# Bias network in steps 1 to 11, masks by the group, 16 transposes of the identity ahead of x

## What is computed

```python
def rel_pos_bias(n, w0, b0, g0, w1, b1, g1, w2, b2, dtype):
    pos = jnp.arange(-n + 1, n, dtype=dtype)[:, None]
    h = jax.nn.silu(ln(pos @ w0 + b0, g0))
    h = jax.nn.silu(ln(h @ w1 + b1, g1))
    h = h @ w2 + b2
    ...
x = x + L0(x, bias=fside_16xSxS, mask=mask_bk0, null_kv=cond, ...)   # layernorm, q/k/v, softmax, Wo, layernorm
x = x + L1(x, bias=rel_pos_bias(...), mask=mask_bf1, ...)            # the same with l2norm of q and k
```

## Time and profile before

| | us |
|---|---|
| median of 3 runs | 1332.85 (1330.36 to 1334.3) |
| the profiled execution | 1334.16 |
| its span | 1332.4 |
| TensorE busy | 1284.4 (96%) |
| VectorE, ScalarE, GpSimd busy | 1101.6, 861.7, 797.3 |

### The profile page before, as it was taken

One profiled execution on the slowest core, in us unless ns is written; L12 is line 12 of the kernel. 1 busy time (PEld: TensorE's weight loads), 2 busy tenths in 40 slices (PEclk: granted clock), 3 DMA queues, 4 the chain that ended last, 5 costly groups with the idle time before them and its releaser, 6 DMA issues.

```text
span 1332.4 us, 28554 instructions
## 1 busy us (share of the span) xinstructions
PE 1284.4 (96%) x8152; PEld 1183.8 (89%) x8152; DVE 1101.6 (83%) x2948; ACT 861.7 (65%) x3246; POOL 797.3 (60%) x1382
## 2 busy tenths in 40 slices
PE   3798999999999999999999999999999999999997
PEld 2587999999999999999999999999999999999995
DVE  5676877877777887887799999899899999999986
ACT  3565667666667777776666766666666666666663
POOL 6443444444445666554567776776766766776673
PEclk8898999999999999999999999999999999999999
DMA  9101411111123212213454101101111110110101
GB/s 286 35 19 50 78 44 47 36 35 47 47 96 111 86 59 96 102 58 112 110 129 174 49 24 47 47 31 39 47 36 34 47 45 26 47 47 24 47 33 40
DMA packets 52195, 85.67 MB, mean 64 GB/s; under 512 B 7888, under 2 KB 22256, under 8 KB 51616
## 3 DMA queue, kind: packets, MB, share of 16 engines
q1 hardware_dynamic: 47168, 75.81, 18.2%
q0 software_dynamic: 4128, 9.03, 2.3%
q10 hardware_dynamic: 832, 0.04, 0.0%
HBM read 57.07 MB, written 27.79 MB: 64 GB/s over the span
## 4 chain that ended last, share of the span: by engine, by line
PE 92%; DVE 3%; issue 2%; ACT 1%; SPq 1%; POOL 1%; DMA 0%; POOLq 0%; DVEq 0%; ACTq 0%
PE bank_q L1270 30%; PE bank_y L1406 26%; PE bank_s L1270 12%; PE bank_o L1270 10%; PE bank_p L1371 6%; PE bank_t L1344 4%; PE bank_t L1310 3%; ACT p_raw L799 1%; PE bank_t L1349 1%; DVE wq_raw L969 1%; PE bank_y L1270 0%; POOL bias L569 0%; SPq L367 0%; DMA bias<-in_fside_16xSxS 0%; DVE pt_l L1152 0%
## 5 line engine op out<-in xcount | busy, mean ns | idle before, releaser
L799 ACT ACTIVATE p_raw<-s_sb,neg_m 128x130 f32<-128x130 f32 (+1 forms) x1024 | 372.0, 366 | 134.7 <-DVE neg_m L1142 133.0
L641 POOL TENSOR_TENSOR p_sb<-p_raw,rden 128x256 f32<-128x256 f32 x256 | 157.6, 615 | 308.3 <-DVE rden L1148 308.3
L1270 PE MATMUL bank_q<-wq_h,xt_h 128*128 128x384 f32 x768 | 268.2, 349 | 4.4 <-DVE xt_l L1040 4.3
L1270 PE MATMUL bank_q<-wq_h,xt_l 128*128 128x384 f32 x768 | 260.0, 339 | 0.0
L1270 PE MATMUL bank_q<-wq_l,xt_h 128*128 128x384 f32 x768 | 259.8, 338 | 0.0
L631 POOL TENSOR_TENSOR bias_g<-bias,mask_row 128x260 f32<-128x260 f32 x256 | 178.5, 697 | 120.7 <-DVE s_sb L1135 119.2
L1406 PE MATMUL bank_y<-wo_h,ot_h 128*128 128x512 f32 x512 | 218.0, 426 | 0.3 <-DVE ot_l L1158 0.3
L1406 PE MATMUL bank_y<-wo_h,ot_l 128*128 128x512 f32 x512 | 201.8, 394 | 0.0
L1406 PE MATMUL bank_y<-wo_l,ot_h 128*128 128x512 f32 x512 | 201.5, 394 | 0.0
L799 ACT ACTIVATION_READ_ACCUMULATOR p_raw<-s_sb,neg_m 128x1 f32 x1024 | 192.5, 188 | 0.0
L1152 DVE TENSOR_TENSOR pt_l<-bank_p,pt_h 128x384 fp32r<-128x384 f32 x256 | 140.6, 549 | 37.4 <-ACT pt_h L806 37.4
(11 more groups left out here) (136 smaller groups left out, 3155.3 us busy)
## 6 DMA issues: line engine op xcount, KB each, us to landing
x_in<-in_x SPq DMA_DIRECT2D x32, 256.0 KB, 3.1
x_res<-in_x SPq DMA_DIRECT2D x32, 256.0 KB, 2.7
x_mid<-y_out SPq DMA_DIRECT2D x32, 256.0 KB, 2.1
x_in<-x_mid SPq DMA_DIRECT2D x32, 256.0 KB, 2.8
x_res<-x_mid SPq DMA_DIRECT2D x32, 256.0 KB, 2.7
out_x<-y_out SPq DMA_DIRECT2D x32, 256.0 KB, 2.1
wq_raw<-in_L_cond_Wq SPq DMA_DIRECT2D x4, 768.0 KB, 6.4
wq_store<-w_sb SPq DMA_DIRECT2D x6, 384.0 KB, 3.9
```

The costliest lines, as they stand in the source:

```text
L641: e.tensor_tensor(to[:, 0:2 * P].rearrange("p (e j) -> p e j", e=2), low_blocks(of)[:, :, 2:LOW], r[:, 0:2, :].broadcast_to([P, 2, P]), AL ...
L799: last = e.activation(p_raw[:, g % 2, lo:hi], s_sb[:, g % 2, lo:hi], ACT.Exp, bias=neg_m[:, h:h + 1], accum_out=esum[:, h:h + 1])
L1270: last = e.matmul(out, a, b, start=(k == 0), stop=(k == len(passes) - 1))
```

## The change

- The bias network leaves the prologue and step 0. Its first layer runs in step 1, norm in 2, silu in 3 and 4 (exp in 3), transposes in 5, product (into `bank_t` now) in 6, second norm in 7, silu in 8 and 9, transposes in 10, table in 11, store in 12. w0, b0 and g0 lie in the upper columns of `wq_raw`, and are loaded once the weights are split. FIRST of layer 0 becomes 13, so that steps 0 to 12 are written out and the loop has steps 13 to 15.
- SP loads the mask ahead of bias0, no network rows ahead of the second x, and the third and fourth x in the prologue.
- GpSimd makes the second rstd ahead of never_seen and the null columns, masks bias0 a group at a time with masked_bias between, and makes the third rstd ahead of groups 2 and 3. Layer 1's null columns move to step 4.
- VectorE takes the second x's statistics and ln_apply around the third part of wq_l, writes the first null key before the splits, and takes the third x's statistics in step 0 (`third_x`).
- The first item's k is transposed into `bank_y` and its second q half into `bank_o`, k first.
- The first projections wait for each chunk of wq_l. wo_l chunks 0 to 3 are VectorE's in two pieces of step 0, chunks 4 to 7 GpSimd's in step 1.
- TensorE transposes the identity 16 times into a bank of scores before the first x.

```diff
-FIRST, LAST = 4, (15, B - 4)
+FIRST, LAST = (13, 4), (15, B - 4)
...
-        w0_b, b0_b, b1_b = row_of(p_raw), row_of(s_sb), wq_raw[:, 0, 0:D]
+        w0_b, b0_b, b1_b = wq_raw[:, 0, D:2 * D], wq_raw[:, 1, D:2 * D], wq_raw[:, 0, 0:D]
...
+        def bank_of_qt(m, half):
+            return bank_o if is_item(m, 0, 0) and half == 1 else bank_t
+        def bank_of_kt(m):
+            return bank_y if is_item(m, 0, 0) else bank_t
...
             load_x((0, 0))
             load_wq(0)
-            for dst, src in ((w0_b, w0[0]), (b0_b, b0), (g_b[0], g0)):
-                net_row(dst, src)
+            load_mask(0)
             load_bias0(0)
             wait(e, xn_ready, (0, 0))
             load_x((0, 1))
             load_bias0(1)
-            load_mask(0)
+            wait(e, xn_ready, (0, 1))
+            load_x((0, 2))
             load_wo(0)
+            net_load(w1_sb[:, :, :], w1.rearrange("(c p) n -> p c n", p=P))
...
+            wait(e, xn_ready, (0, 2))
+            load_x((0, 3))
             for p in range(3):
-                e.wait_ge(wq_ready[p], 1)
+                e.wait_ge(wq_ready[p], KC)
+            for dst, src in ((w0_b, w0[0]), (b0_b, b0), (g_b[0], g0)):
+                net_row(dst, src)
...
             load_small()
+            inverse_deviations(item_of(-2))
             never_seen()
             e.wait_ge(null_bias_loaded, 16 * LAYERS)
             place_nulls(0)
-            place_nulls(1)
-            mask_bias0()
-            inverse_deviations(item_of(-2))
+            mask_bias0(0)
+            masked_bias((0, 0), 0)
+            mask_bias0(1)
             masked_bias((0, 0), 1)
-            net_deviation(VE1)
-            masked_bias((0, 0), 0)
+            inverse_deviations(item_of(-1))
+            mask_bias0(2)
+            mask_bias0(3)
             masked_bias((0, 0), 2)
-            inverse_deviations(item_of(-1))
...
+            def third_x(m):
+                if is_item(m, 0, 0):
+                    x_stats((0, 2))
+                    means_variances(item_of(-1))
+            def net_part(m):
+                if is_item(m, 0, 1):
+                    net_first_layer()
+                if is_item(m, 0, 2):
+                    net_norm(RSTD1, CEN1, g_b[0])
+                if is_item(m, 0, 3):
+                    net_silu(EXP1, PLUS1, REC1, [0, 1])
+                if is_item(m, 0, 4):
+                    net_silu(EXP1, PLUS1, REC1, [2, 3])
+                if is_item(m, 0, 6):
+                    net_stats(PRE2, ST2, MV2)
...
                 on(0, maxima, 1)
+                on(0, third_x)
                 on(0, sums, 0)
...
                 on(1, split_qt, 0)
-                on(0, net_second_silu, [0, 1])
+                on(0, net_part)
                 on(0, split_pt, 1)
-                on(0, start_output)
                 on(3, x_stats)
                 on(0, sums, 3)
                 on(1, split_qt, 1)
                 on(0, split_pt, 2)
+                on(0, start_output, [0, 1])
...
             project_weights(0, 1)
-            project_weights(0, 2)
             x_stats(second)
             means_variances(item_of(-2))
+            project_weights(0, 2)
+            ln_apply(second)
+            first_null()
+            null_key(0)
             take_mask(first)
-            net_first_layer()
-            first_null()
             q_scale_out(first, 2)
-            ln_apply(second)
             split_qt(first, 0)
-            net_norm(RSTD1, CEN1, g_b[0])
+            split_kt(first)
             split_qt(first, 1)
-            net_silu(EXP1, PLUS1, REC1, [0])
-            split_kt(first)
-            x_stats(third)
-            means_variances(item_of(-1))
-            net_silu(EXP1, PLUS1, REC1, [1, 2, 3])
...
                 for c in range(KC):
-                    passes += [(xt_h[:, c, :], wq_h[:, c, lo:hi]), (xt_h[:, c, :], wq_l[:, c, lo:hi]),
+                    if is_item(m, 0, 0):
+                        e.wait_ge(wq_ready[p], c + 1)
...
+                    for b, done in ((6, TCOPY1), (7, PRE2), (11, TCOPY2), (12, TABLE)):
+                        if is_item(m, 0, b):
+                            e.wait_ge(net_step, done)
...
+            def idle_transposes(n):
+                for _ in range(n):
+                    e.transpose(bank_s[1][:, 0:P], ident[:, :], ident[:, :])
             first = (0, 0)
+            idle_transposes(16)
             transpose_x(first)
             for p in range(3):
                 project(first, p)
             transpose_q(first, 0)
+            transpose_k(first)
             transpose_q(first, 1)
-            transpose_k(first)
             stream(e, step)
```

More of the change, by code:

```diff
@@ L430, in bulk @@
                     for half in range(2):
[L431 removed]
+                        e.wait_ge(wo_ready[half], 4)
                     load_wo(1)
@@ L471, in _ @@
             net_load(b2_col[:, :], b2.rearrange("(h a) -> h a", a=1))
-            wait(e, xn_ready, (0, 1))
-            load_x((0, 2))
-            for layer in range(LAYERS):
-                e.dma_start(g_out_sb[:, layer, :], row(g_out[layer]).broadcast_to([P, D])).then_inc(g_out_loaded, 16)
             load_mask(1)
@@ L741, in project_weights, with output_weights @@
                         .then_inc(wq_h_ready[p], 1)
-            def output_weights(layer, half):
+            def output_weights(first):
                 e.wait_ge(wo_loaded, 16)
-                for c in range(4 * half, 4 * half + 4):
+                for c in range(first, first + 2):
                     e.activation(wo_h[:, c, :], wo_raw[:, c, :], ACT.Copy).then_inc(wo_h_ready, 1)
@@ L935, in project_weights, with output_weights @@
                                                   op0=ALU.mult, op1=ALU.subtract)
-                last.then_inc(wq_ready[p], 1)
-            def output_weights(layer, half):
-                for c in range(4 * half, 4 * half + 4):
+                    last.then_inc(wq_ready[p], 1)
+            def output_weights(layer, half, chunks):
+                for c in chunks:
                     e.wait_ge(wo_h_ready, OC * layer + c + 1)
-                    last = e.tensor_tensor(wo_l[:, c, :], wo_raw[:, c, :], wo_h[:, c, :].bitcast(F32), ALU.subtract)
-                last.then_inc(wo_ready[half], 1)
+                    e.tensor_tensor(wo_l[:, c, :], wo_raw[:, c, :], wo_h[:, c, :].bitcast(F32), ALU.subtract)\
+                        .then_inc(wo_ready[half], 1)
             def net_stats(pre, st, mv):
@@ L1326, in project @@
                     wait(e, q_done[0], m)
-                passes = []
                 for c in range(KC):
-                    passes += [(xt_h[:, c, :], wq_h[:, c, lo:hi]), (xt_h[:, c, :], wq_l[:, c, lo:hi]),
-                               (xt_l[:, c, :], wq_h[:, c, lo:hi])]
-                product(bank_q[p % 2][:, 0:hi - lo], passes).then_inc(q_psum[p], 1)
+                    if is_item(m, 0, 0):
+                        e.wait_ge(wq_ready[p], c + 1)
+                    for k, (a, b) in enumerate(((xt_h, wq_h), (xt_h, wq_l), (xt_l, wq_h))):
+                        last = e.matmul(bank_q[p % 2][:, 0:hi - lo], a[:, c, :], b[:, c, lo:hi],
+                                        start=(c == 0 and k == 0), stop=(c == KC - 1 and k == 2))
+                last.then_inc(q_psum[p], 1)
             def transpose_q(m, half):
```

180 lines of the change are left out of this document (94 added, 86 removed).

## The result

The changed kernel's median is 1321.98 us (4 executions, 1320.64 to 1324.1) beside 1333.42 for the kernel before on the same chip (1330.36 to 1334.3). The ratio is 0.9917, 95% interval 0.99 to 0.9935: faster by 0.83%. The forecast was 1320.4 us. The profiled execution took 1324.1 us with a span of 1322.2 us; the one before had 1334.16 and 1332.4.

A forecast was written before the change was run, and what follows sets the result against it. TensorE was taken to bound the body, with what the opening loses lost for good. Gains of 7.8 up to step 0, 3.8 in step 0 and 0.9 in steps 1 to 12 sum to 12.5 us: 1320.4, range 1313 to 1328.

The forecast's parts named there:

- The two waits of TensorE: Opening: TensorE idles for wq_l's third part behind the second x's statistics, and 5.1 us for step 0's first P.
- Piece 1: Time up to step 0: it opens near 26.6 us instead of 34.44, a gain of 7.8 us.
- The landing: Opening: the second x's load lands at 19.3 us, bounds 15 and 20.3, where it had landed at 20.26.
- The whole wait from 21.4 to 27.54: Opening: time from the second x's statistics to its xn, which the change was to remove by making rstd earlier.
- Piece 2: Step 0: GpSimd becomes the bound; step 1 opens at 53.7 us, 3.8 us more gain, 11.6 in all.
- Piece 3: Steps 1 to 12: loss of 11.7 us against 12.6 before, so 0.9 us more gained.
- a piece costs its length less the cover of 1.47: VectorE's network pieces between q split and second pt_l: a piece of X us costs X - 1.47, sum 4.2 us.
- From step 13 on the instructions are the same: Step 13 to the end: nothing changes, so the gain is what step 13's start moves by, 12.5 us.
- The first: Opening: second x lands near 15 us or the clock stays up in both gaps; gain 16 to 20, 1314.5 us; chance 0.13.
- The second: Steps 0 and 1: GpSimd and VectorE hold each other up, 3.7 us; gain 5.5, 1327.4 us; chance 0.18.
- The third: Full steps: every moved piece costs its whole length, 9.3 of 11.6 us are given back; 1330.5 us; chance 0.10.
- The fourth: Nine steps now straight code wait for their instructions; with 2 us a step slower, 1338 us; chance 0.05.

The follow-up runs named there:

- before_rstd_first: Kernel before, with only GpSimd's second rstd moved ahead of the null columns and bias masks: 1335.06 us, ratio 1.0009.
- no_idle: Changed kernel without the 16 idle transposes of the identity: 1321.24 us, ratio 0.9903.
- pool_masks_first: Changed kernel with GpSimd's masks of bias0 groups 2 and 3 ahead of the third x's rstd: 1319.45 us, ratio 0.988.
- x_ahead: Changed kernel with the second x loaded ahead of the mask and of bias0: 1318.31 us, ratio 0.9892.
- clock_fill: Changed kernel with 24 more identity transposes ahead of the first item's third projection and 34 ahead of step 0's first P: 1319.23 us, ratio 0.989.
- best_order: Changed kernel, masks 2 and 3 before third rstd, second x's statistics after third weight part, layer 1's bias in step 29, loop from step 15: 1315.43 us.

## Why the prediction was right, point by point

The two waits of TensorE that the sum named are in the trace. Its total was 12.5 us, the traces' spans differ by 10.2 (1332.4 to 1322.2) and the medians by 11.4, and it comes out near partly by luck: terms missed in both directions.

**Piece 1**: 7.8 forecast, 9.19 measured. Three terms were off.
- The landing: 19.3 taken, 18.12 measured, 1.2 us of gain, which is luck. The same issue order gave 18.0 to 20.5, and the kernel before gave 20.26 and, in before_rstd_first, 18.07. Nor was the load issued 2.4 us earlier, but 1.05 (9.54 instead of 10.59): the issue of the mask took 2.33 us where the first network row's had taken 2.27 in the same place, and not the 0.89 of its old place. In three of the ten traces the issue came at 10.80 to 11.06, behind an issue of bias0 that took 2.5 to 3.3 us instead of 1.6.
- From the landing to the end of the third part: 5.4 taken, 4.6 measured (18.12 to 22.69). The low clock was taken for all twelve matmuls, and they took 2.7 us instead of 3.8.
- From there to step 0: 1.9 taken, 2.56 measured, with two of the transposes at the slow pace (1.05 and 0.93 us).

The idle transposes were taken at 0, and no_idle shows 0. The row's bound, 1.3 us from a first projection at full clock, did not come about.

One reading under this piece was wrong. "The whole wait from 21.4 to 27.54" was not one wait for rstd: VectorE waited 1.77 us for the mask, then made the network's first layer and small copies, and waited 1.17 for rstd. The prediction names the mask as bytes in the queue and never as something that VectorE waits for, though the change moves its load ahead of bias0, and before_rstd_first shows that it held VectorE until 23.49 when rstd did not. The sum came to no harm, because it started anew from the landing of x.

**Piece 2**: 3.8 forecast for step 0, 4.82 measured. From step 0's start to the third x's variance 5.5 us were taken and 5.4 measured, to the first P 6.4 and 5.9, TensorE's gap was 5.1 and 4.06. The clock was then 0.50 from 36 to 42 us, as taken. pool_masks_first shows that GpSimd's order was the bound, as the prediction said.

**Piece 3**: steps 1 to 12 were to lose 11.7 us and lost 11.66 (299.36 - 51.30 is 248.06, less 12 times 19.70). The silu halves, steps 3, 4, 8 and 9, lost 0.72, 1.02, 0.72 and 1.04; the rule "a piece costs its length less the cover of 1.47" had given 0.7, 1.0, 0.7 and 1.0. But the near hit of the total is partly luck. Step 1 lost 2.4 us, where 3.4 were forecast: 2.6, and 0.8 for the first layer, which is in that step. TensorE's own work for the network cost 0.9 more than the 4.9 of the sum: step 6, with the product, took 23.16 (22.8 by the sum), step 5 lost 0.80 (0.44), step 11 1.13 (0.95) and step 10 0.44 (0.44).

**The step that failed** is the sentence "From step 13 on the instructions are the same. So the change is worth what step 13's start moves by". The instructions are the same, but in step 13 what lies beside them isn't: the table's store moved from step 3 to step 12, and TensorE lost up to 2.8 us in step 13. The sum took the store at nothing. The reload of step 31 was on the edge before (20.82 and 21.03 us), and took 21.0 to 23.9 in the changed order; there not even the neighbours had moved, and the cause of the difference stays open. Both together, with step 30, took 4.4 us of the 14.95 in the profiled execution.

**The rivals.** The first (x near 15, or the clock stays up: 1314.5) didn't happen in the changed kernel, but x_ahead and clock_fill made its two halves: 1318.31 and 1319.23. Each was worth less than was said, the early landing since bias0 is next. The second (VectorE and GpSimd hold each other up) is there in the rows, but small, and outside of steps 0 and 1's waits: rstd took 1.02 us beside wq_l's third part, and 0.72 in best_order, where that part was done. VectorE's pair of one-column kt_l took longer as well, changed kernel, then best_order:

```profile
22.32 1.04 DVE L1138 TENSOR_TENSOR kt_l<-null_kn,kt_h 64x1 fp32r<-64x1 f32 x2
```

```profile
22.70 0.32 DVE L1138 TENSOR_TENSOR kt_l<-null_kn,kt_h 64x1 fp32r<-64x1 f32 x2
```

The 1.04 lies beside GpSimd's addition of the causal mask, 0.68 us from 22.27. The 0.32 lies beside GpSimd's four short copies (1.06 us from 22.03), ahead of its first mask at 23.17. The first fits the Trainium skill, "SBUF — State Buffer", SBUF: two separate sides, by which the engine that comes second on the shared port pair waits for the whole instruction of the first. By it GpSimd's copies, which read SBUF too, could have cost something as well; they cost nothing that the row shows. The 3.7 us of the rival would have needed ten such meetings on the path. The third (every piece costs its whole length) is refuted by the silu steps. The fourth (straight code slower in steps 4 to 12) is too: steps 2 and 7 took 19.71.

## What to carry to other kernels

An idle time that a trace puts down to one wait may be the last of several holds: before_rstd_first removed the wait for rstd, the wait for the mask grew from 1.77 to 4.23 us, and nothing was gained. So look at every wait and every piece of work between the arrival of the data and its use. When work with a large transfer is moved, look at the steps where the transfer now lands and at every other transfer there, even if not one instruction of the step has changed. And an engine that opens a kernel in order should do first what can be done with what has already landed: masks ahead of a late variance and weights ahead of a late x, with two smaller edits, brought 6.4 us more beside the 11.4 of the change.

## What was not expected of the hardware

- 58 transposes of the identity held TensorE's granted clock at 1.00 through two gaps of 5.0 and 4.1 us (clock_fill). With 16 ahead of x the next four transposes were fast in 5 of 11 traces, but never the first projection.
- The same load in the same issue order landed between 18.0 and 20.5 us from execution to execution: issued at 9.4 to 9.6 us it landed at 18.0 to 19.7 in seven traces, issued at 10.8 to 11.1 at 19.6 to 20.5 in three. Two single traces can't be compared in the opening without these numbers.
- TensorE stood 0.6 to 2.6 us with nothing missing that the profile shows, in the step after a 2 MB store was issued, always from the same place in the step to about the store's landing, in 5 of 11 traces, and not at all in the other 6.
- An issue on SP's queue that takes 0.43 us took 4.25 us beside the table's and the weights' stores, and 2.5 to 3.3 us beside the table's alone.
